# Decoder layer on one core: the feed-forward's first batches prepared inside the last two attention steps

## The reference

```
x = x + local_attention(layernorm(x))          # 16 heads of 8, windows of 64 and the window before
x = x + cross_attention(layernorm(x), ctx)     # 16 heads of 8, 256 keys
x = x + ffn(layernorm(x))

def act_quant(x):   # int8 grid, one scale per token
    scale = 127.0 / clip(max(abs(x), -1), 1e-5)
    return clip(round(x * scale), -128, 127) / scale
def bit_linear(x, w):           # w on the grid -1, 0, 1 times mean(abs(w))
    return act_quant(x) @ weight_quant(w).T
h = bit_linear(x, w1)                          # 128 -> 512
h = silu(depthwise_conv1d(h, conv_w, conv_b))  # 3 taps along the tokens
out = bit_linear(h, w2)                        # 512 -> 128
```

## Time and profile before

| what | us |
|---|---|
| median of 3 runs | 339.83 (338.51 to 340.8) |
| the profiled execution | 339.14 |
| its span, first to last instruction | 337.4 |
| mean granted TensorE clock | 0.94 of full |

### The profile page before, as it was taken

One profiled execution on the slowest core, in us unless ns is written; L12 is line 12 of the kernel. 1 busy time (PEld: TensorE's weight loads), 2 busy tenths in 40 slices (PEclk: granted clock), 3 DMA queues, 4 the chain that ended last, 5 costly groups with the idle time before them and its releaser, 6 DMA issues. The chain is left out here.

```text
span 337.4 us, 8544 instructions
## 1 busy us (share of the span) xinstructions
PE 284.5 (84%) x3298; PEld 182.0 (54%) x3298; DVE 230.3 (68%) x562; ACT 164.8 (49%) x329; POOL 134.9 (40%) x216
## 2 busy tenths in 40 slices
PE   0903967999997999999999999999897179999993
PEld 0702646777776777776566555565443134544451
DVE  7758942676774767899677786787111349999864
ACT  1310052456465555558677766767784023332331
POOL 5642086738557458458685300000000453344100
PEclk9965795999999999999999999999999569999998
DMA  7269376674468644564653633000000000000001
GB/s 259 61 163 253 117 175 165 135 183 108 111 171 230 137 112 100 142 142 95 147 132 71 150 75 93 3 3 1 3 0 2 0 0 2 17 23 16 18 23 31
DMA packets 20135, 30.96 MB, mean 92 GB/s; under 512 B 2812, under 2 KB 17532, under 8 KB 18432
## 3 DMA queue, kind: packets, MB, share of 16 engines
q1 hardware_dynamic: 19368, 29.99, 35.8%
q10 hardware_dynamic: 728, 0.44, 0.5%
HBM read 16.53 MB, written 13.63 MB: 89 GB/s over the span
## 5 line engine op out<-in xcount | busy, mean ns | idle before, releaser
L607 DVE TENSOR_REDUCE negm<-ps 128x2 bf16<-128x512 f32 (+1 forms) x192 | 123.2, 690 | 55.6 <-PE ps L255 22.1
L492 ACT ACTIVATE probs<-ps 128x512 f32<-128x512 f32 x192 | 105.2, 610 | 37.0 <-PE ps L293 25.8
L282 PE MATMUL ps<-QT,KT 98*128 98x512 bf16 x128 | 47.6, 383 | 4.7 <-ACT probs L492 4.2
L247 PE MATMUL ps<-KT,QT 97*128 97x256 bf16 x256 | 47.5, 272 | 1.0 <-DMA KT<-stack_parts 0.5
L973 PE MATMUL ps<-tapw,xqT 128*128 128x512 f32 x96 | 45.5, 611 | 0.0
L1139 POOL TENSOR_TENSOR ve<-mv,eps 128x2 f32<-128x2 f32 x8 | 1.6, 195 | 89.6 <-DVE mv L1049 89.6
L247 PEld LDWEIGHTS ps<-KT,QT 97*128 97x128 bf16 x256 | 23.8, 98 | 15.5 <-DVE negm L607 2.8
L317 PE MATMUL ps<-probs,V 128*32 128x256 f32 x512 | 30.9, 382 | 0.7 <-ACT probs L492 0.7
L973 PEld LDWEIGHTS ps<-tapw,xqT 128*128 128x128 f32 x96 | 18.9, 197 | 16.9 <-issue 16.4
L776 POOL TENSOR_SCALAR_AFFINE_SELECT probs<-probs 128x512 f32<-128x512 f32 x32 | 21.2, 662 | 16.0 <-ACT probs L492 16.0
L1022 ACT ACTIVATE probs<-ps 128x512 f32<-128x512 f32 x16 | 9.6, 598 | 35.9 <-PE ps L973 35.9
(11 more groups left out here) (134 smaller groups left out, 496.7 us busy)
## 6 DMA issues: line engine op xcount, KB each, us to landing
stack_parts<-high SPq DMA_DIRECT2D x32, 192.0 KB, 3.3
QT<-stack_parts SPq DMA_DIRECT2D x16, 384.0 KB
KT<-stack_parts SPq DMA_DIRECT2D x8, 768.0 KB
stack_parts<-mid SPq DMA_DIRECT2D x32, 128.0 KB
stack_parts<-low SPq DMA_DIRECT2D x32, 64.0 KB, 2.1
CT<-in_ctx_t_dram SPq DMA_DIRECT2D x1, 1024.0 KB, 10.0
out_dram<-probs SPq DMA_DIRECT2D x16, 64.0 KB, 1.5
X<-in_xp_dram SPq DMA_DIRECT2D x1, 768.0 KB, 5.7
```

Of the source, the lines that this page charges most:

```text
L247: last = nc.tensor.matmul(o[:, j * S:(j + 1) * S], QT[r, s, j, pr, e * S + t * P:e * S + (t + 1) * P], KT[r, s, pr, e, :], start=True, sto ...
L282: last = nc.tensor.matmul(o.rearrange("p (j q) -> p j q", j=2), KT[r, s, pr, e, kt * P:(kt + 1) * P], QT[r, s, :, pr, e * S:(e + 1) * S], ...
L492: nc.scalar.activation(probs[:, k, :], bank(n % 3), ACT.Exp, scale=SCALE).then_inc(s_exp, 1)
L607: nc.vector.tensor_reduce(dst, src, AX.X, ALU.max, negate=True).then_inc(m_max, 1)
```

## The change

The second block is gone; its steps stand in the first one, with semaphores of their own (f_ before the name), other PSUM banks (up in 5, 3 and 4, x turned in 3, 4 and then 0, h in 1 and 2, down in 6 and 7) and in this order:

- DVE, step 14: statistics 0 and 1 in beat 4, x_scales(0) in beat 9, x_finish(0) and x_scales(1) in beat 12. Step 15: x_finish(1) and statistics 2 in beat 0, x_scales(2) and statistics 3 in beat 7, x_finish(2) in beat 11. From then on it is three batches ahead.
- POOL: its feed-forward steps follow step 15's (empty) work.
- PE: x_turn(0) in beat 14 of step 14; in step 15 the opening of up(0) in beat 3, its taps in beats 4, 6 and 8, x_turn(1) in beat 5.
- ACT: x_copy(0) and x_copy(1) behind the exponentials 0 and 7 of step 15.
- The tail of unit 15 is woven into units 1 to 3.

```diff
+                        if i == UNITS - 2 and k == 14:
+                            ffn_x_turn(0)
+                        if i == UNITS - 1:
+                            if k == 3:
+                                ffn_up_open(0)
+                            if k in (4, 6, 8):
+                                ffn_up_tap(0, (k - 4) // 2)
+                            if k == 5:
+                                ffn_x_turn(1)
...
                 u = UNITS - 1
                 pv(u, 1, bank(BX))
+                ffn_up(1)
                 pe.wait_ge(y_done, u)
                 o_turn(u, bank(BY))
+                h_turn(0)
+                ffn_up(2)
                 oT_turn(u, bank(BY)).then_inc(xT_ps, 1)
+                ffn_down(0)
+                ffn_x_turn(2)
+                h_turn(1)
                 pe.wait_ge(xT_sb, UNITS + 7)
                 project(u, UNITS % 6, bank(BY))
+                for n in range(3, NU):
+                    ffn_up(n)
+                    ffn_down(n - 2)
+                    if n % TPB == 0 and n // TPB + 1 < B:
+                        ffn_x_turn(n // TPB + 1)
+                    h_turn(n - 1)
+                ffn_down(NU - 2)
+                h_turn(NU - 1)
+                ffn_down(NU - 1)
...
+                def ffn_down(u):
+                    pe.wait_ge(hT_sb, u + 1)
+                    if u >= 2:
+                        pe.wait_ge(o_ready, u - 1)
+                    if u == 1:
+                        pe.wait_ge(y_done, UNITS)
...
                 u = UNITS - 1
+                silu(0)
                 o_copy(u, bank(BX))
+                silu(1)
+                h_copy(0)
+                silu(2)
                 ox_copy(UNITS + 6, bank(BY), 0, S)
+                x_copy(2)
+                h_copy(1)
+                for n in range(3, NU):
+                    silu(n)
+                    if n % TPB == 0 and n // TPB + 1 < B:
+                        x_copy(n // TPB + 1)
+                    h_copy(n - 1)
+                h_copy(NU - 1)
...
+                def ffn_x_stats(b):
+                    v.wait_ge(y_done, B + b + 1)
+                    if b >= 2:
+                        v.wait_ge(f_normed, b - 1)
+                    else:
+                        v.wait_ge(normed, UNITS)
...
+                def ffn_ahead(i, k):
+                    at = 16 * (i - UNITS + 2) + k
+                    if at == 4:
+                        ffn_x_stats(0)
+                        ffn_x_stats(1)
+                    if at == 9:
+                        x_scales(0)
+                    if at == 12:
+                        x_finish(0)
+                        x_scales(1)
+                    if at == 16:
+                        x_finish(1)
+                        ffn_x_stats(2)
+                    if at == 16 + 7:
+                        x_scales(2)
+                        ffn_x_stats(3)
+                    if at == 16 + 11:
+                        x_finish(2)
...
-                u = UNITS - 1
-                norm(u, bank(BY))
-                residual(u, bank(BY))
+                for n in range(NU):
+                    b = n // TPB
+                    if n % TPB == 0:
+                        if b + 3 < B:
+                            x_scales(b + 3)
+                    elif b + 4 < B:
+                        ffn_x_stats(b + 4)
+                    h_scales(n)
+                    h_quantise(n)
+                    if n == 0:
+                        norm(UNITS - 1, bank(BY))
+                    if n >= 2:
+                        finish(n - 2)
+                    if n == 2:
+                        residual(UNITS - 1, bank(BY))
+                    if n % TPB == 1 and b + 3 < B:
+                        x_finish(b + 3)
+                finish(NU - 2)
+                finish(NU - 1)
```

More of the change, by code:

```diff
@@ L360, in project, with ffn_x_turn, ffn_up_open @@
                     last.then_inc(y_ps, 1)
+                def ffn_x_turn(b):
+                    pe.wait_ge(x_quant, b + 1)
+                    if b >= 3:
+                        pe.wait_ge(f_xT_sb, b)
+                    o = bank(XT_FIRST[b] if b < 2 else XT)
+                    for t in range(TPB):
+                        last = nc.tensor.transpose(o[:, t * P:(t + 1) * P], xs[:, b % 2, t, :], identf[:])
+                    last.then_inc(f_xT_ps, 1)
+                def ffn_up_open(u):
+                    o = bank(UP[u % 3])
+                    pe.wait_ge(f_xT_sb, u // TPB + 1)
+                    if u == 0:
+                        pe.wait_ge(s_pf, 9)
+                    if u >= 3:
+                        pe.wait_ge(act_done, u - 2)
+                    nc.tensor.matmul(o, onesb[:], bias3[:, 2 * D:2 * D + FH], start=True, stop=False, skip_group_check=True)
@@ new lines, in ffn_up_tap, with ffn_up @@
+                def ffn_up_tap(u, k):
+                    b, t = u // TPB, u % TPB
+                    last = nc.tensor.matmul(bank(UP[u % 3]), xqT[:, b % 2, t * P + k:t * P + k + P], tapw[:, k, :],
+                                            start=False, stop=(k == 2), skip_group_check=True)
+                    if k == 2:
+                        last.then_inc(up_ps, 1)
+                def ffn_up(u):
+                    ffn_up_open(u)
+                    for k in range(3):
+                        ffn_up_tap(u, k)
@@ new lines, in h_turn @@
+                def h_turn(u):
+                    pe.wait_ge(h_quant, u + 1)
+                    if u >= 2:
+                        pe.wait_ge(hT_sb, u - 1)
+                    for n in range(NB):
+                        last = nc.tensor.transpose(bank(HT[u % 2], BF16)[:, n * P:(n + 1) * P],
+                                                   hq[:, u % 2, n * P:(n + 1) * P], identb[:])
+                    last.then_inc(hT_ps, 1)
+                def ffn_down(u):
+                    pe.wait_ge(hT_sb, u + 1)
+                    if u >= 2:
+                        pe.wait_ge(o_ready, u - 1)
+                    if u == 1:
+                        pe.wait_ge(y_done, UNITS)
+                    for n in range(NB):
+                        last = nc.tensor.matmul(bank(DOWN[u % 2])[:, 0:D], hT[:, u % 2, n, :], w2T[:, n, :],
+                                                start=(n == 0), stop=(n == NB - 1))
+                    last.then_inc(down_ps, 1)
@@ L514, in ox_copy, with x_copy, silu, h_copy @@
                     nc.scalar.copy(oxT[:, n % 6].rearrange("p a t -> p (a t)")[:, lo:hi], src[:, lo:hi]).then_inc(xT_sb, 1)
+                def x_copy(b):
+                    act.wait_ge(f_xT_ps, b + 1)
+                    if b == 0:
+                        act.wait_ge(padded, 1)
+                    if b >= 2:
+                        act.wait_ge(up_ps, TPB * (b - 1))
+                    nc.scalar.copy(xqT[:, b % 2, 1:S + 1], bank(XT_FIRST[b] if b < 2 else XT)[:, 0:S]).then_inc(f_xT_sb, 1)
+                def silu(u):
+                    act.wait_ge(up_ps, u + 1)
+                    if u == 0:
+                        act.wait_ge(pv_ps, 2 * UNITS - 1)
+                    if u >= 3:
+                        act.wait_ge(h_rounded, u - 2)
+                    nc.scalar.activation(hid[:, u % 3, :], bank(UP[u % 3]), ACT.Silu).then_inc(act_done, 1)
+                def h_copy(u):
+                    act.wait_ge(hT_ps, u + 1)
+                    if u >= 2:
+                        act.wait_ge(down_ps, u - 1)
+                    nc.scalar.copy(hT[:, u % 2].rearrange("p n s -> p (n s)"),
+                                   bank(HT[u % 2], BF16)[:, 0:FH]).then_inc(hT_sb, 1)
                 def iteration(i):
@@ L530, in iteration @@
                             ox_copy(i + 6, bank(BY), 0 if i >= 1 else S, 2 * S if i + 6 < UNITS else S)
+                        if i == UNITS - 1 and k in (0, 7):
+                            x_copy(k // 7)
                 def row(u):
@@ L634, in iteration, with finish @@
+                def finish(u):
+                    v.wait_ge(down_ps, u + 1)
+                    if u >= 4:
+                        v.wait_ge(o_sent[u % 4], 16 * (u // 4))
+                    nc.vector.scalar_tensor_tensor(out=ob[:, u % 4, :], in0=bank(DOWN[u % 2])[:, 0:D],
+                                                   scalar=hrs[:, u % 4:u % 4 + 1], in1=X[:, u, :],
+                                                   op0=ALU.mult, op1=ALU.add).then_inc(o_ready, 1)
                 def iteration(i):
@@ L713, in _ @@
                 link(nc.vector.memset(V[:, 1, :, 0:4:3, HD:HD + 1], 1.0))
+                nc.vector.memset(xqT[:, :, 0:1], 0.0)
+                nc.vector.memset(xqT[:, :, S + 1:S + 2], 0.0).then_inc(padded, 1)
                 for n in range(max_end(-1)):
@@ L868, in _ @@
                     iteration(i)
+                ffn_normalise(0)
+                ffn_normalise(1)
+                x_round(0)
+                x_round(1)
+                for b in range(2, B):
+                    ffn_normalise(b)
+                    x_round(b)
             @block.sync
```

306 lines of the change are left out of this document (95 added, 211 removed).

## The result

The changed kernel takes 323.28 us (median of 4, 322.65 to 324.95) against 340.05 (338.51 to 340.8): a ratio of 0.952, 95% interval 0.947 to 0.957. The forecast was 322.9.

The account below looks back on a forecast made before the run. The prediction took the seam before the feed-forward to be bound by a preparation chain's latency. Saving 16.9 (16.4 less 0.8 plus 1.3) from the 337.4 span gave 320.5; with 1.74 and 0.69 added, 322.9 us, range 319.5 to 327.3.

Parts of the forecast that it names:

- Part 1: Feed-forward preparation moved into the last two attention steps on DVE and POOL: price 0, x_turn(0) with a margin of 1.0.
- Part 2: up(0) and two x turns between PE's last attention beats: 0.27 exposed in step 14 and 1.36 in step 15.
- Part 3: First SiLU and its 1.28 us table load ahead of the last o_copy on ACT: price 0.
- Part 4: Last attention tail among units 1 to 3: up(3) starts at 268.9, and waiting for the residual costs PE 0.8.
- Part 5: x prepared three batches ahead: x_turn waits go, DVE bounds to unit 8, then PE; up(15) ends at 313.4.
- 1.3 won: Gain between up(3) and the end, through missing x_turn waits and a DVE rid of x sooner.
- Rival A: PE is full in step 15, so the overlap is dearer: 3.4 more, 326.3 us; chance 0.20.
- B: Cheaper: the beats' taps fill the waits fully (-1.0) and port clashes vanish (-0.9), 321.0 us; chance 0.15.
- C: Slower than before: the granted clock stays low in the feed-forward, 2.0 a unit, up to 353 us; chance 0.02.
- D: x_turn(0) held by a wait until after the last residual, so the seam stays: 1.5 saved, 338.3 us; chance 0.03.
- the median's 0.69: Amount by which the median of three runs lay above the profiled execution, added to 322.2 to forecast 322.9.

Follow-up runs that it names:

- e2: The changed kernel with up(0) alone moved from the beats of step 15 to behind the last P·V half; 327.62 us.
- e3: The changed kernel with the last residual on DVE ahead of the h chain of unit 2 instead of behind finish(0); 324.54 us.
- e1: The changed kernel's one block without the barrier, but every feed-forward step in the old order behind the last residual; 339.59 us, ratio 1.001 to the kernel before.
- e4: The changed kernel with x prepared two batches ahead in the loop, as before, not three; 327.52 us.
- e10: The changed kernel with the last attention tail done first, as before, and units 1 and on behind it; 327.58 us.
- e5: The changed kernel with x_finish on POOL instead of DVE; 321.95 us, and 322.58 in a second set.
- e7: The kernel before with 20 unread matmuls on PE at the start of the second block; 339.67 us, ratio 1.001.
- e9: The kernel before with 28 unread matmuls on PE at the start of the second block; 337.61 us (one run).

## Why the prediction was right, point by point

The forecast's times, counted from the mark of before (237.51), beside those of the changed kernel from its own (239.70):

| | forecast | measured |
|---|---|---|
| last P·V half starts | 21.6 | 21.80 |
| first SiLU starts | 22.85 | 23.06 |
| up(3) starts | 31.4 | 32.04 |
| h chain 8 ends | 56.2 | 56.77 |
| up(15) ends | 75.9 | 76.66 |
| end | 83.0 | 83.50 |

The range of 319.5 to 327.3 holds 323.28, and the sum of the savings can be followed from point to point: 16.4, less 0.8, plus 1.3, is 16.9 by forecast; measured are 16.2 when up(1) starts, 1.2 lost by up(3) and 1.4 won by the end, 16.4.

- Part 1, price 0: right. x_turn(0) waited for nothing, with 1.1 us to spare (1.0 forecast).
- Part 2: 1.63 exposed by forecast (0.27 in step 14 and 1.36 in step 15), 21.80 - 19.95 = 1.85 measured (0.22 and 1.63). e2 shows that of up(0) alone 1.4 to 1.5 are hidden.
- Part 3, price 0: right. The load starts 0.02 behind the last exponential and the SiLU stands right behind its 1.28; the drain of 1.38 that the Trainium skill adds ("ScalarE: Activation LUTs", What ACT_TABLE_LOAD costs) does not show in this case, and the measurement decides.
- Part 4: the PE waits were 0.50 (hq) and 0.41 (residual) where 0.3 and 0.8 had been worked out. e3 shows that the residual's isn't on the path. The forecast calls it a cost to PE, but its end is counted from DVE's slots behind that residual, so the wait never entered the sum (35.0 from the mark by forecast, its successor starts at 274.87 - 239.70 = 35.17). This is the loosest step: up(3) is 0.64 late, and only 0.17 of that reaches DVE.
- Part 5: the order, DVE to unit 8 and PE from there, is what the chain shows. The slot of an odd unit was undersized, 3.80 for 3.93: beside hq the instruction ahead of it (L820) also runs into POOL, 0.72 for 0.49. That is the term that was mis-sized: 0.13 in each of the odd slots of units 3, 5 and 7, 0.4 of the 0.57 by which h chain 8 is late. Behind up(15), 0.76 late, the forecast took the rest as unchanged at 7.05; it took 6.84, since the last `down` met the full clock: 0.2 of luck. The barrier's part in the sum, 0.4, is confirmed by e1.
- "1.3 won" through the missing x_turn waits and a DVE that is rid of x sooner: 1.4 on the forecast's own points, as above. What the third batch of lead is worth by itself, e4 measures at 2.1 by the last SiLU.
- Rival A falls by e2. B didn't come: the beats hid less than forecast, not more, and the clashes with POOL grew by one. C has nothing for it: the clock stayed at 1.00. e10 shows how near it is, though: an order that left PE idling in turns lost 1.7 to the clock. D falls by x_turn(0) at 247.93, ahead of the last residual.
- The forecast had taken the median's 0.69 over the profiled execution along. The profiled execution of the changed kernel was the slowest of its four instead, by time lost before the mark; that the medians agree to 0.4 us is partly luck. So is the base: the forecast took over the 0.5 that the last projection lost to the clock in the profile of the kernel before.

## What to carry to other kernels

A seam between stages costs the latency of the first stage's preparation, and it is worth moving only as much of it as idle engines can take: here the preparation was free, the first matmuls between beats were hidden to about half, and the barrier itself was worth 0.4 us. Behind the seam ask which engine's slot sum is larger than the old critical engine's: removing a wait of PE (e3) won nothing while DVE was the bound, and 0.39 less on DVE in each batch won 1.36 by the last SiLU (e5), until PE was the bound. Compare variants from a mark that all of them share; the stretch repeated to 0.05 us where whole runs differed by 3. Then look at the granted clock inside it: 0.5 of the kernel before's stretch, and 0.2 to 0.4 of some variants', were matmuls that met the lower clock in one execution and not in another.

## What the runs showed of the hardware that was not expected

- The granted clock fell after PE had been busy again: in e7 the turn of x behind 2.10 us of idling still ran at the full clock (1.00 from 271.5 to 272.4 us), and only from 272.9 on was it 0.50, with the taps already running. With 0.39 us of idling at that place (e9) it stayed at 1.00. When it falls isn't fixed by the instructions: with the same ones ahead, it was 0.77 and 0.50 at the last projection in the kernel before and 1.00 in e1, e7 and e9.
- POOL took 0.90 us a tile of 128x128 to subtract a constant and multiply by a per-partition scalar, and 0.36 to multiply by such a scalar and add a constant. Both pairs in e5's timeline:

```profile
285.07 0.72 POOL L986 TENSOR_SCALAR xr<-xn,xm 128x128 f32<-128x128 f32 x2 [1.59 <-DVE xm L792]
285.90 1.79 POOL L996 TENSOR_SCALAR xs<-xr,xrs 128x128 f32<-128x128 f32 x2
```

- Two profiled executions of one kernel differed by 2.95 us before the mark, with the same instructions in the same order. From 40 to 60 us the changed kernel's first profile had a granted clock of 0.69 where its second had 0.91, but by 60 us that was nearly made good: the same instructions start only 0.17 later in it. 0.9 more came between 100 and 108 us, at a clock of 1.00 in both, and 1.8 between 124 and 137 us; there the first profile had a clock of 0.57 from 127 to 131 us and the second one 1.00. What caused the 0.9 was not looked into.
